# Attention weights cast to bf16 in DRAM first, and loaded by SP's queue instead of GpSimd's

## The chip, the cores and the metric

One Trainium2 chip, all 8 cores. Each core runs the same program on its own data: core 2b + half computes 1024 of the 2048 tokens of batch element b, and reads the whole sequence for keys and values. There is no traffic between cores. The metric is the device time of one execution in microseconds, that of the slowest core; lower is better.

## The reference

One adaLN transformer layer on x of shape (4, 2048, 2048), float32, 16 heads of 128, MLP of 8192 with ternary weights and 8-bit activations:

```python
mod = (_silu(L0_c) @ L0_wmod).reshape(L0_c.shape[0], 6, 1, -1)
sa, ca, ga, sb, cb, gb = (mod[:, 0], ..., mod[:, 5])
ga = (2 * (ga >= 0) - 1) * jnp.maximum(jnp.abs(ga), 0.25)      # gb likewise
h = _layernorm(x, axis=-1) * (1 + ca) + sa
x = x + ga * attn(h, wq, wk, wv, wo)      # rope on q and k, softmax over 2048 keys, y @ wo.T
h = _layernorm(x, axis=-1) * (1 + cb) + sb
x = x + gb * ffn(h, w1, w2, w3)
# ffn: bitlinear(h, w) = rmsnorm, activations rounded to 8 bits by their row's maximum,
#      weights rounded to -1, 0, 1 by the mean of |w|;
#      silu(bitlinear(h, w1)) * bitlinear(h, w2), then bitlinear(., w3)
```

## The kernel before

The kernel is written by hand, engine by engine. `st(engine, fn, waits, inc)` (L63) appends an instruction to the engine's list; `waits` are semaphores with the value to wait for, `inc` is what it raises when done. The five lists run in the order in which they were written (L81). VectorE (DVE) and ScalarE (ACT) also count every instruction of their own (sVE, sSE), sMM counts finished groups of matmuls. A DMA is issued by SyncE (its queue is SPq in the profile, the hardware queue q1) or by GpSimd (POOL, the software queue q0); a wait holds all that stands behind it on the same engine. In this kernel every DMA that changes float32 into bf16 is issued by POOL, all others by SP.

The stages, in order:

1. POOL issues 16 loads of x (xc, 1 MB of float32 each, cast into h_sb, L289), then the first weight loads. DVE meanwhile makes the rope tables.
2. Modulation (L369 to L412): for j in 24 groups of 512 columns of wmod, 16 loads of 256 KB (L378) go into the ring mring, which has two halves of 8 loads; TensorE multiplies them in float32 (L396), DVE picks the diagonal (L408, L411). A half is loaded again when its matmuls are done.
3. First layer norm over 4 blocks of tokens (L440 to L508): sums on TensorE, the rows sent round by a bounce through DRAM on SP (`bounce`, L230), DVE and ACT write h into h_sb.
4. 16 heads, in the order of `events` (L609): V of two heads ("V", g), then ("KQ", 2g), ("KQ", 2g+1). Event i uses slot i % 2 (wsl or wsl2, 8 KB per partition). The load of event i + 2 (`emit_ev_load`, L623) waits until the last matmul of event i is done; it is written right behind that event's matmuls, L682 and L760. After K and Q of head h (L692, L728; the copy out on ACT, L704 and L738) comes `emit_scale(24)` (L574, called at L772): 24 chunks of 512 KB of w1, w2 or w3, each loaded by SP in two DMAs (L592) into one of three slots (halves of wfl, rbc), and summed by ACT as |w| (L599); 16 x 24 chunks are all three matrices. Then the attention of the head: scores (L795), exp on ACT (L806), sums and P V (L779, L785). A chunk's load waits for ACT's sum of the chunk three before it.
5. The softmax sums go through DRAM and are spread to all partitions, one load per head into rbc or sm2 (L846), and DVE scales ysb (L854).
6. Output projection for 16 blocks dc of 128 outputs (L888): SP loads the block of x into xst (L892), the weights come by `emit_wo_load` (L874) into two slots, the load of dc + 2 waits for wo_done[dc], the last statistics matmul (L937) of block dc. 2 x 16 matmuls (L902), ACT scales (L911), DVE adds x (L917) and casts (L921), TensorE sums x and its square (L933, L937), SP spills the block (x2s, L946).
7. Second layer norm, quantization, the MLP with w1, w2 (L1184, L1195), and w3 (L1396). These parts load their weights on SP.

Of the kernel before, what the change touches and what calls it, by code (L numbers as in the profile page):

```python
# [7 lines left out]
BF16 = mybir.dt.bfloat16  # L8
# [6 lines left out]
NKC = D // 128  # L15
# [27 lines left out]
class Bld:  # L43
# [19 lines left out]
    def st(self, eng, fn, waits=(), inc=None, inck=1):  # L63
        ser = self.serial.get(eng)
        if ser is not None:
            waits = tuple(waits) + ((ser, ser.n),)
            inc, inck = ser, 1
        waits = tuple((s.h, v) for (s, v) in waits if v > 0)
        if inc is not None:
            inc.inc(inck)  # L70

        def run(e, fn=fn, waits=waits, inc=inc, inck=inck):
            for h, v in waits:
                e.wait_ge(h, v)
            r = fn(e)
            if inc is not None:
                r.then_inc(inc.h, inck)
        self.q[eng].append(run)
        return inc.n if inc is not None else None
# [12 lines left out]
def build(nc, dbg=(), phases=99, e_head=0):  # L92
    dbg = set(dbg)
    K = Bld(nc)
    st = K.st
# [3 lines left out]
    cvec_d = nc.dram_tensor("cvec", [128, NKC], F32, kind="ExternalInput").ap()  # L99
    pos_d = nc.dram_tensor("pos", [1, T], F32, kind="ExternalInput").ap()  # L100
    wmod_d = nc.dram_tensor("wmod", [24, 128, NKC, 512], F32, kind="ExternalInput").ap()
    wq_d = nc.dram_tensor("wq", [NH, 128, NKC, 128], F32, kind="ExternalInput").ap()
    wk_d = nc.dram_tensor("wk", [NH, 128, NKC, 128], F32, kind="ExternalInput").ap()
    wv_d = nc.dram_tensor("wv", [8, 128, NKC, 256], F32, kind="ExternalInput").ap()
    wo_d = nc.dram_tensor("wo", [NKC, 128, NKC, 128], F32, kind="ExternalInput").ap()
# [87 lines left out]
    sM1 = K.sem("sM1")  # L193
    sST0 = K.sem("sST0")
    sST1 = K.sem("sST1")
    sB = [K.sem("sB%d" % i) for i in range(6)]
    sVE = K.sem("sVE")
    sSE = K.sem("sSE")
    sMM = K.sem("sMM")
# [40 lines left out]
    def emit_ladder(chains):  # L240
# [31 lines left out]
        out=t_ang[:, :], in_=pos_d[0:1, :].broadcast_to((64, T))), inc=sLD, inck=16)  # L272
# [15 lines left out]
    for kc in range(NKC):  # L288
        st("gpsimd", lambda e, kc=kc: e.dma_start(  # L289
            out=h_sb[:, kc * T:(kc + 1) * T], in_=xc[kc * 128:(kc + 1) * 128, :]),  # L290
           inc=sXL, inck=16)
    w_xall = sXL.n

    st("scalar", lambda e: e.activation(out=tab[:, 2:3], in_=tab[:, 1:2], func=AF.Ln),
       waits=[(sVE, w_consts)])
# [13 lines left out]
    for k in [256.0, 128.0, 64.0, 32.0, 16.0, 8.0, 4.0, 2.0, 1.0]:  # L309
# [27 lines left out]
       waits=[(sVE, w_sinin)])  # L337
# [285 lines left out]
    def emit_ev_load(ev):  # L623
        i = ev_index[ev]
        sl = slot_of[ev]
        sA = sAs[sl]
        wcred = [(sMM, ev_done[events[i - 2]])] if i >= 2 else []
        if i == 1:
            wcred = wcred + [(sSE, w_cos)]
        if ev[0] == "V":  # L630
            g = ev[1]
            st("gpsimd", lambda e, sl=sl, g=g: e.dma_start(
                out=slots[sl][:, 0:4096], in_=wv_d[g]), waits=wcred, inc=sA, inck=16)
        else:
            h = ev[1]
            st("gpsimd", lambda e, sl=sl, h=h: e.dma_start(
                out=slots[sl][:, 0:2048], in_=wk_d[h]), waits=wcred, inc=sA, inck=16)
            st("gpsimd", lambda e, sl=sl, h=h: e.dma_start(
                out=slots[sl][:, 2048:4096], in_=wq_d[h]), inc=sA, inck=16)
        ev_ld[ev] = sA.n  # L640

    emit_ev_load(events[0])
# [231 lines left out]
    def emit_wo_load(dc):  # L874
        sl = dc % 2
        sA = sAs[sl]
        st("gpsimd", lambda e, dc=dc, sl=sl: e.dma_start(
            out=wo_slot[sl], in_=wo_d[dc]),
           waits=[(sMM, wo_done[dc - 2])] if dc >= 2 else
                 [(sMM, ev_done[events[-2 + dc]])], inc=sA, inck=16)  # L880
        ev_ld[("WO", dc)] = sA.n

    emit_wo_load(0)
# [617 lines left out]
```

How the kernel before makes its waits and increments, by code:

```python
        def run(e, fn=fn, waits=waits, inc=inc, inck=inck):  # L72
            for h, v in waits:
                e.wait_ge(h, v)
            r = fn(e)
            if inc is not None:
                r.then_inc(inc.h, inck)
```

## Time and profile before

| what | us |
|---|---|
| timed runs, median of 2 (8291.23 to 8309.24) | 8300.23 |
| the profiled execution's own time | 8325.77 |
| its span on the slowest core (cores: 8259.1 to 8324.2) | 8324.2 |
| TensorE / VectorE / ScalarE / GpSimd busy | 3580.1 / 2874.6 / 3055.9 / 38.9 |
| moved by DMA | 706.67 MB |

The span is the time from the first to the last instruction of core 1 in one profiled execution. Busy times of the engines overlap each other; a matmul's end is modelled. Times below are counted from the span's start. "x16" behind a row says that so many instructions were merged, and a bracket tells how long the engine was idle before it and what released it. GB/s and MB count the bytes that are written, so a cast from float32 counts half of what it reads.

### The profile page before, as it was taken

The numbers are of one execution on the slowest core, as the hardware profiler recorded it, in microseconds if no ns is written. First come the engines' busy times: TensorE is split into PE (matmuls) and PEld (weight loads), VectorE is DVE, ScalarE is ACT, GpSimd is POOL, SyncE is SP. The second block draws the span as 40 slices with busy tenths as digits, with TensorE's granted clock in tenths as the row PEclk, the third lists the DMA queues.
The fourth block names the chain that finished last, engine by engine and source line by source line (L and its number), as shares of the span: only waits on it lengthen the run. The fifth ranks groups of instructions, "written<-read, shape, count | busy, mean of one in ns | idle before, by whom it ended". The sixth has DMA issues, their size and how long they took to land.

```text
span 8324.2 us, 57853 instructions; the slowest of 8 cores (8259.1 to 8324.2 us)
## 1 busy us (share of the span) xinstructions
PE 3580.1 (43%) x12896; PEld 1437.6 (17%) x12896; DVE 2874.6 (35%) x4177; ACT 3055.9 (37%) x4011; POOL 38.9 (0%) x76
## 2 busy tenths in 40 slices
PE   4872454545364436003565656651111111154544
PEld 1330222212221112001222222220000000011111
DVE  4225211122121211584333333336666666411111
ACT  0003343343334411264333333334555555422222
POOL 0000000000000000000000000000000000000000
PEclk9775787778787767556777778775555555576677
DMA  7650424243324423201222222211011111133333
GB/s 196 196 150 16 122 86 126 77 129 100 108 80 130 124 73 84 71 1 46 82 89 84 87 86 85 90 62 33 31 34 32 33 34 31 62 104 107 104 106 106
DMA packets 442896, 706.67 MB, mean 85 GB/s; under 512 B 50307, under 2 KB 197766, under 8 KB 441472
## 3 DMA queue, kind: packets, MB, share of 16 engines
q1 hardware_dynamic: 432192, 661.04, 25.6%
q0 software_dynamic: 10368, 41.95, 2.9%
q8 instruction: 114, 1.87, 0.1%
q14 instruction: 222, 1.82, 0.1%
HBM read 693.97 MB, written 50.51 MB: 89 GB/s over the span
## 4 chain that ended last, share of the span: by engine, by line
ACT 24%; DVE 24%; DMA 20%; PE 16%; issue 9%; SPq 5%; DVEq 1%; ACTq 1%
DMA wfl<-w 13%; DVE sm L256 6%; ACT tmpb L250 6%; PE ps L396 5%; PE ps L1396 4%; ACT esb L806 4%; PE ps L665 3%; DMA rbc<-w 3%; DVE ternB L1167 2%; PE ps L902 2%; ACT sgntmp L1160 2%; ACT terntmp L1153 2%; ACT sgntmp L1157 2%; ACT sgntmp L1162 2%; ACT terntmp L1365 1%
## 5 line engine op out<-in xcount | busy, mean ns | idle before, releaser
L1396 PE MATMUL ps<-q3c,ternA 128*128 128x512 bf16 x2048 | 766.8, 553 | 1934.1 <-DVE ternA L1373 1934.0
L250 ACT ACTIVATE tmpb<-sm,consts 128x512 f32<-128x512 f32 x1120 | 808.4, 722 | 173.5 <-DVE sm L256 119.4
L256 DVE SCALAR_TENSOR_TENSOR sm<-tmpb,sm 128x512 f32<-128x512 f32 x1120 | 774.5, 692 | 206.8 <-ACT tmpb L250 135.6
L1184 PE MATMUL ps<-q,ternA 128*128 128x512 bf16 x2048 | 570.7, 448 | 360.7 <-DVE ternB L1167 360.7
L1396 PEld LDWEIGHTS ps<-q3c,ternA 128*128 128x128 bf16 x2048 | 255.7, 130 | 2445.2 <-issue 2396.6
L1365 ACT ACTIVATE terntmp<-wfl,wsc 128x512 f32<-128x512 f32 x256 | 184.7, 721 | 1144.0 <-DMA wfl<-w 1051.2
L795 PE MATMUL ps<-qsb,ksb 128*128 128x512 bf16 x512 | 209.3, 420 | 900.1 <-ACT esb L806 811.9
L1373 DVE TENSOR_TENSOR ternA<-terntmp,sgntmp 128x512 bf16<-128x512 f32 x256 | 177.3, 693 | 1191.3 <-ACT sgntmp L1370 1191.3
L396 PE MATMUL ps<-mring,smt 128*128 128x512 f32 x768 | 431.1, 731 | 149.5 <-DVE smt L388 131.4
L1195 PE MATMUL ps<-q,ternB 128*128 128x512 bf16 x2048 | 452.5, 379 | 0.0
L1164 DVE TENSOR_TENSOR ternA<-terntmp,sgntmp 128x2048 bf16<-128x2048 f32 x64 | 146.7, 2293 | 797.5 <-ACT sgntmp L1157 735.3
L819 DVE COPY rows<-ps 1x512 f32<-1x512 f32 x32 | 21.7, 679 | 1114.7 <-PE ps L795 836.9
L599 ACT ACTIVATE wfl<-wfl 128x1024 f32<-128x1024 f32 x256 | 270.4, 1056 | 325.0 <-DMA wfl<-w 317.8
L806 ACT ACTIVATE esb<-ps,consts 128x512 bf16<-128x512 f32 x512 | 351.8, 687 | 79.8 <-PE ps L795 36.5
L1234 PE MATMUL ps<-sqb,onesb 128*128 128x512 bf16 x128 | 74.8, 584 | 685.5 <-ACT sqb L1226 685.5
L1184 PEld LDWEIGHTS ps<-q,ternA 128*128 128x128 bf16 x2048 | 228.6, 113 | 690.9 <-issue 530.4
L1153 ACT ACTIVATE terntmp<-wfl,wsc 128x2048 f32<-128x2048 f32 x64 | 128.1, 2002 | 581.9 <-DMA wfl<-w 575.1
L665 PE MATMUL ps<-wsl,h_sb 128*128 128x256 bf16 x2048 | 262.1, 275 | 136.0 <-DVE vsb L676 89.9
L704 ACT ACTIVATE kraw<-ps 128x512 f32<-128x512 f32 x64 | 38.2, 597 | 598.9 <-PE ps L692 398.6
L692 PE MATMUL ps<-h_sb,wsl 128*128 128x512 bf16 x1024 | 231.3, 379 | 51.6 <-ACT kraw L704 51.6
L1195 PEld LDWEIGHTS ps<-q,ternB 128*128 128x128 bf16 x2048 | 200.4, 98 | 241.6
L795 PEld LDWEIGHTS ps<-qsb,ksb 128*128 128x128 bf16 x512 | 51.2, 102 | 1099.1 <-issue 1093.5
(199 smaller groups left out, 4612.0 us busy)
## 6 DMA issues: line engine op xcount, KB each, us to landing
wfl<-w SPq DMA_DIRECT2D x1024, 256.0 KB, 4.5
mring<-wmod SPq DMA_DIRECT2D x384, 256.0 KB, 4.6
rbc<-w SPq DMA_DIRECT2D x256, 256.0 KB, 4.5
wfl<-w SPq DMA_DIRECT2D x512, 128.0 KB, 2.3
q3c<-q3s SPq DMA_DIRECT2D x384, 128.0 KB, 2.2
xst<-x2s SPq DMA_DIRECT2D x32, 512.0 KB, 3.8
hs<-hch SPq DMA_DIRECT2D x128, 128.0 KB, 1.7
hch<-hs SPq DMA_DIRECT2D x128, 128.0 KB, 2.4
```

What stands on the lines that cost most here:

```text
L250: sws[j] = st("scalar", lambda e, ch=ch, src_u=src_u: e.activation(out=ch["bb"], in_=src_u, func=AF.Sign, bias=consts[:, 8:9]), waits=[(sV ...
L256: e.scalar_tensor_tensor(out=ch["tb"], in0=ch["bb"], scalar=-(k / 2.0), in1=src_u, op0=ALU.mult, op1=ALU.add),
L396: st("tensor", lambda e, j=j, kc=kc, kk=kk, hs=hs, sl2=sl2: e.matmul(psE[:, :], sl2, mring[:, (hs % 2) * 4096 + kk * 512: (hs % 2) * 4096 ...
L599: "scalar", lambda e, slot=slot, col=col: e.activation(out=slot, in_=slot, func=AF.Abs, accum_out=accw[:, col:col + 1]),
L665: st("tensor", lambda e, kkc=kkc, kc=kc, sl=sl_v: e.matmul(psE[:, 0:256], h_sb[:, kc * T + kkc * 128: kc * T + kkc * 128 + 128], slots[sl] ...
L795: qslot=qslot: e.matmul(ps_s[:, 0:512], kslot[:, kkc * 128:(kkc + 1) * 128], qslot[:, qh * 512:(qh + 1) * 512], start=True, stop=True),
L806: w_exp[(h, qh, kkc)] = st("scalar", lambda e, kkc=kkc, ps_s=ps_s: e.activation(out=esb[:, kkc * 512:(kkc + 1) * 512], in_=ps_s[:, 0:512], ...
L1153: st("scalar", lambda e, wslc1=wslc1: e.activation(out=terntmp[:, :], in_=wslc1[:, :], func=AF.Sign, bias=wsc[:, 6:7]), waits=[(sW, w_wld) ...
L1184: e.matmul((psU0 if th == 0 else psU1)[:, 0:512], tA[:, kc * 128:(kc + 1) * 128], q12[:, kc * OWN + th * 512: kc * OWN + (th + 1) * 512], ...
L1195: st("tensor", lambda e, th=th, kc=kc, tB=tB: e.matmul((psC if th == 0 else psD)[:, 0:512], tB[:, kc * 128:(kc + 1) * 128], q12[:, kc * OW ...
L1365: st("scalar", lambda e, wslc=wslc: e.activation(out=terntmp[:, 0:512], in_=wslc[:, 0:512], func=AF.Sign, bias=wsc[:, 6:7]), waits=[(sW, w ...
L1396: tsl=tsl: e.matmul(psx[:, 0:512], tsl[:, di * 128:(di + 1) * 128], qsl[:, th * 512:(th + 1) * 512], start=(k3 == 0), stop=(k3 == NFC - 1)),
```

## The change

All attention weights are first cast to bf16 by DMAs from DRAM to DRAM: 56 casts, issued by POOL right behind the loads of x, into four new DRAM tensors. The loads of the weights into SBUF are then plain bf16 loads, issued by SP, and each of them waits for all 56 casts (sPC) as well as for its slot. They are written at the same places as before, so on SP they now stand between the instructions that SP already had there.

```diff
+    wvbf_d = nc.dram_tensor("wvbf", [8, 128, 4096], BF16, kind="Internal").ap()
+    wkbf_d = nc.dram_tensor("wkbf", [16, 128, 2048], BF16, kind="Internal").ap()
+    wqbf_d = nc.dram_tensor("wqbf", [16, 128, 2048], BF16, kind="Internal").ap()
+    wobf_d = nc.dram_tensor("wobf", [16, 128, 2048], BF16, kind="Internal").ap()
...
@@ -290,6 +295,25 @@
     w_xall = sXL.n
+
+    def _pc(dst, srcv):
+        st("gpsimd", lambda e, dst=dst, srcv=srcv: e.dma_start(out=dst, in_=srcv),
+           inc=sPC, inck=16)
+        pc_n[0] += 1
+
+    for g in range(8):
+        _pc(wvbf_d[g], wv_d[g])
+        for h in (2 * g, 2 * g + 1):
+            _pc(wkbf_d[h], wk_d[h])
+            _pc(wqbf_d[h], wq_d[h])
+    for dc in range(NKC):
+        _pc(wobf_d[dc], wo_d[dc])
@@ -624,19 +648,20 @@
-        wcred = [(sMM, ev_done[events[i - 2]])] if i >= 2 else []
+        wcred = ([(sMM, ev_done[events[i - 2]])] if i >= 2 else []) + \
+                [(sPC, 16 * pc_n[0])]
         if i == 1:
             wcred = wcred + [(sSE, w_cos)]
         if ev[0] == "V":
             g = ev[1]
-            st("gpsimd", lambda e, sl=sl, g=g: e.dma_start(
-                out=slots[sl][:, 0:4096], in_=wv_d[g]), waits=wcred, inc=sA, inck=16)
+            st("sync", lambda e, sl=sl, g=g: e.dma_start(
+                out=slots[sl][:, 0:4096], in_=wvbf_d[g]), waits=wcred, inc=sA, inck=16)
         else:
             h = ev[1]
-            st("gpsimd", lambda e, sl=sl, h=h: e.dma_start(
-                out=slots[sl][:, 0:2048], in_=wk_d[h]), waits=wcred, inc=sA, inck=16)
-            st("gpsimd", lambda e, sl=sl, h=h: e.dma_start(
-                out=slots[sl][:, 2048:4096], in_=wq_d[h]), inc=sA, inck=16)
+            st("sync", lambda e, sl=sl, h=h: e.dma_start(
+                out=slots[sl][:, 0:2048], in_=wkbf_d[h]), waits=wcred, inc=sA, inck=16)
+            st("sync", lambda e, sl=sl, h=h: e.dma_start(
+                out=slots[sl][:, 2048:4096], in_=wqbf_d[h]), inc=sA, inck=16)
@@ -874,10 +899,11 @@
-        st("gpsimd", lambda e, dc=dc, sl=sl: e.dma_start(
-            out=wo_slot[sl], in_=wo_d[dc]),
-           waits=[(sMM, wo_done[dc - 2])] if dc >= 2 else
-                 [(sMM, ev_done[events[-2 + dc]])], inc=sA, inck=16)
+        st("sync", lambda e, dc=dc, sl=sl: e.dma_start(
+            out=wo_slot[sl], in_=wobf_d[dc]),
+           waits=([(sMM, wo_done[dc - 2])] if dc >= 2 else
+                  [(sMM, ev_done[events[-2 + dc]])]) +
+                 [(sPC, 16 * pc_n[0])], inc=sA, inck=16)
```

Three places, as the built programs have them (lines of the changed kernel are some 5 to 26 higher than those of the kernel before). First POOL's list at the start. Before:

```order
L289 DMA h_sb<-xc 128x2048 x16
L632 DMA wsl<-wv 128x4096
L636 DMA wsl_100<-wk 128x2048 [waits sSE]
L638 DMA wsl_100<-wq 128x2048
L636 DMA wsl<-wk 128x2048 [waits sMM]
```

And now:

```order
L294 DMA h_sb<-xc 128x2048 x16
L303 DMA wvbf<-wv 32x16384
L303 DMA wkbf<-wk 16x16384
L303 DMA wqbf<-wq 16x16384
L303 DMA wkbf<-wk 16x16384
L303 DMA wqbf<-wq 16x16384
L303 DMA wvbf<-wv 32x16384
```

wsl_100 is the second slot, wsl2. The loads into the slots are gone from POOL, and the casts stand in their place without any wait, each as 16 or 32 runs of 16384 elements.

Second, SP's list between the attention of one head (L822, now L847, sends its sums out) and the scale chunks of the next (L592, now L616), where the next head is an even one. Before:

```order
L592 DMA rbc<-w 128x512 [waits sSE]
L592 DMA rbc<-w 128x512
L822 DMA bnc<-rows 1x1024 [waits sVE]
L592 DMA wfl<-w 128x512 [waits sSE]
L592 DMA wfl<-w 128x512
L592 DMA wfl<-w 128x512 [waits sSE]
```

And now:

```order
L616 DMA rbc<-w 128x512 [waits sSE]
L616 DMA rbc<-w 128x512
L847 DMA bnc<-rows 1x1024 [waits sVE]
L661 DMA wsl_100<-wkbf 128x2048 [waits sMM,sPC]
L663 DMA wsl_100<-wqbf 128x2048
L657 DMA wsl<-wvbf 128x4096 [waits sMM,sPC]
L616 DMA wfl<-w 128x512 [waits sSE]
L616 DMA wfl<-w 128x512
L616 DMA wfl<-w 128x512 [waits sSE]
```

Weight loads that wait for matmuls (sMM) of V and of K and Q now stand ahead of the first scale chunks; before an odd head it is one such load pair.

Third, SP's list in the output projection. Before:

```order
L892 DMA xst<-xc 128x1024 [waits sVE,sXS0]
L946 DMA x2s<-xst 128x1024 [waits sVE]
L892 DMA xst<-xc 128x1024 [waits sVE,sXS1]
L946 DMA x2s<-xst 128x1024 [waits sVE]
L892 DMA xst<-xc 128x1024 [waits sVE,sXS0]
```

And now:

```order
L918 DMA xst<-xc 128x1024 [waits sVE,sXS0]
L902 DMA wsl<-wobf 128x2048 [waits sMM,sPC]
L972 DMA x2s<-xst 128x1024 [waits sVE]
L918 DMA xst<-xc 128x1024 [waits sVE,sXS1]
L902 DMA wsl<-wobf 128x2048 [waits sMM,sPC]
L972 DMA x2s<-xst 128x1024 [waits sVE]
```

A wo load with a wait for TensorE now stands ahead of each spill and of the next load of x.

## Rows read from the trace of the kernel before

**Rows 1.** The page: busy time by engine; the chain that ended last.

```profile
PE 3580.1 (43%) x12896; PEld 1437.6 (17%) x12896; DVE 2874.6 (35%) x4177; ACT 3055.9 (37%) x4011; POOL 38.9 (0%) x76
ACT 24%; DVE 24%; DMA 20%; PE 16%; issue 9%; SPq 5%; DVEq 1%; ACTq 1%
```

**Rows 2.** Stages: length, busy of PE, PEld, DVE, ACT, POOL, PEclk, DMA share, GB/s.

```profile
86.00:587.00 501.00, 436.52 (x787) 169.76 (x787) 143.61 (x437) 3.24 (x8) 0.54 (x2) 0.79 0.65 195
587.00:815.00 228.00, 54.44 (x109) 12.75 (x109) 117.18 (x156) 94.10 (x130) 0.00 (x0) 0.52 0.05 14
```

**Rows 3.** Waits (total us, times, longest), and the landing of loads into wsl.

```profile
PE ps L396 <- DMA mring<-wmod: 18.0, 6, 4.4
...
POOL wsl L636 <- PE ps L665: 1661.6, 8, 773.1
...
DMA to landing us min/median/max: 5.1/7.1/69.0
```

**Rows 4.** DMA at the start: queues 10 to 70 us (packets, MB, share); mring loads to 75 us; h_sb loads.

```profile
q0 software_dynamic: 2101, 7.72, 75.2%
q1 hardware_dynamic: 2091, 4.11, 27.3%
...
mring<-wmod SPq DMA_DIRECT2D x16, 256.0 KB, 39.7
...
L289 POOL DMA_DIRECT2D h_sb<-xc x16: 535/606/662, 1.6 to 9.5; - x16
DMA to landing us min/median/max: 7.8/35.8/62.8
```

**Rows 5.** Chain of the modulation stage; the line of its matmuls.

```profile
265.89 18.39 PE ps L396 x32
286.75 18.39 PE ps L396 x32
...
L396 PE MATMUL ps<-mring,smt x768: 592/698/1193, 86.0 to 579.9; 128*128 128x512 f32 x192
```

**Rows 6.** DMA issues from 200 to 580 us: KB each, median us to landing.

```profile
mring<-wmod SPq DMA_DIRECT2D x279, 256.0 KB, 4.5
```

**Rows 7.** Timeline at the end of the first layer norm.

```profile
815.36 1.80 PE L665 MATMUL ps<-wsl,h_sb 128*128 128x256 bf16 x7 [45.69 <-ACT tab L509]
```

**Rows 8.** One head's scale chunks: timeline; two stretches (columns as rows 2); sums in wfl.

```profile
2342.10 0.53 POOL L636 DMA_DIRECT2D wsl<-wk  x1 [129.86 <-PE ps L728]
2342.63 1.06 ACT L599 ACTIVATE wfl<-wfl 128x1024 f32<-128x1024 f32 x1
2351.46 1.06 ACT L599 ACTIVATE wfl<-wfl 128x1024 f32<-128x1024 f32 x1 [5.20 <-DMA wfl<-w]
2394.37 2.26 ACT L806 ACTIVATE esb<-ps,consts 128x512 bf16<-128x512 f32 x3
...
2341.60:2394.30 52.70, 1.01 (x2) 0.14 (x2) 3.50 (x7) 28.17 (x49) 1.15 (x2) 0.53 0.77 229
2370.00:2376.00 6.00, 0.00 (x0) 0.00 (x0) 0.00 (x0) 3.45 (x6) 0.00 (x0) 0.50 0.83 267
...
L599 ACT ACTIVATE wfl<-wfl x256: 1056/1056/1057, 887.7 to 2907.9; 128x1024 f32<-128x1024 f32 x128
```

**Rows 9.** Output projection: timeline of block 0 into 1; landing and waits for xst.

```profile
3042.35 6.57 PE L902 MATMUL ps<-ysb,wsl 128*128 128x512 bf16 x16 [94.55 <-DVE ysb L854]
3060.54 0.33 SPq L892 DMA_DIRECT2D xst<-xc  x1
3061.89 0.53 POOL L877 DMA_DIRECT2D wsl<-wo  x1 [199.90 <-PE ps L937]
3067.57 0.69 DVE L917 TENSOR_TENSOR xst<-xst,kraw 128x512 f32<-128x512 f32 x1 [7.86 <-ACT kraw L911]
...
DMA xst<-xc: 29.9, 4
...
DMA to landing us min/median/max: 2.6/4.0/7.3
```

More of the change, by code:

```diff
@@ L195, in build @@
     sST1 = K.sem("sST1")
+    sPC = K.sem("sPC")
     sB = [K.sem("sB%d" % i) for i in range(6)]
@@ L292, in build @@
     w_xall = sXL.n
+    pc_idx = {}
+    pc_n = [0]
+    def _pc(dst, srcv):
[4 more added lines that the diff above has]
+        _pc(wvbf_d[g], wv_d[g])
+        pc_idx[("V", g)] = pc_n[0]
+        for h in (2 * g, 2 * g + 1):
+            _pc(wkbf_d[h], wk_d[h])
+            _pc(wqbf_d[h], wq_d[h])
+            pc_idx[("KQ", h)] = pc_n[0]
+    for dc in range(NKC):
+        _pc(wobf_d[dc], wo_d[dc])
+        pc_idx[("WO", dc)] = pc_n[0]
     st("scalar", lambda e: e.activation(out=tab[:, 2:3], in_=tab[:, 1:2], func=AF.Ln),
```

## The prediction

> **What bounds the kernel now.** I read the shares of the engines and the chain that ended last, then the waits by engine, then the stages one by one, and last the DMA rows of the stages that the change touches. No engine carries the span: TensorE is busy for 43% of it, and the chain runs through ACT, DVE, DMA and PE in turn [rows 1]. What counts is which wait ends last in each stage. Of the stages, the change touches the modulation matmuls (86 to 587 us) with the layer norm behind them (587 to 815) [rows 2], the heads (815 to 3042, the weight scales among them) [rows 7, 9], and the output projection (3042 to 3323). The 5001 us behind them (8324 less 3323: MLP and what leads to it) keep their instructions.
>
> The question to ask first is whether anybody waits for the loads that are changed. In the list of what TensorE waits for [rows 3] no row names a load of wsl; the only DMA in it is mring, with 18.0 us. Turned round, it is POOL that waits for TensorE to free a slot, for the K loads alone 1661.6 us behind V's matmuls [rows 3]. Such a load lands in 7.1 us (median) [rows 3] and is asked for two events ahead. Making it cheaper can't shorten a wait that isn't there. What can change is the traffic that the casts add, and what the loads do to the queue into which they are moved.
>
> **Part 1: 56 casts from DRAM to DRAM at the start.** They write 8 x 2 MiB / 2 + 48 x 0.5 MiB = 32 MiB = 33.55 MB of bf16 and read twice that. Price per MB: from 10 to 70 us the old kernel does nearly nothing on its DMA engines but the same kind of transfer (xc cast into h_sb). There the software queue moved 7.72 MB in 75.2% of 16 engines' time [rows 4], so 60 x 0.752 / 7.72 = 5.84 us of all 16 engines per MB. The casts cost 33.55 x 5.84 = 196 us of all 16. They queue behind the 16 xc loads, the last of which is issued at 9.5 us and lands 62.8 us later, at 72 [rows 4]; the wv load that came next (69.0 us to landing) is gone. The matmuls begin at 86.0 us, so some 13 us or 2.2 MB are free; 31.3 MB (183 us) are left, beside the loads of wmod.
>
> That stage has no room for 183 us. One j (16 loads of 256 KB, 4.19 MB; the matmuls of 16 k-chunks) takes 20.86 us: it starts at 265.89, the next at 286.75 [rows 5]. The DMA engines are 0.65 busy meanwhile [rows 2]. The ring holds only one j ahead, so loads that come too slowly stop TensorE. How the two queues share is shown from 10 to 70 us too: beside the casts the hardware queue got 27.3% and moved 4.11 MB in 60 us [rows 4], against 12.1 MB that the stage wants in that time. By these rates the casts need 31.3 / 7.72 x 60 = 243 us, in which wmod advances by 243 x 4.11 / 60 = 16.7 MB, 4.0 j, where it made 243 / 20.86 = 11.7 before. Lost: 7.7 x 20.86 = 160 us. The other end of sharing is that the wmod loads get nearly nothing while a cast is there: the order of the changed kernel shows each cast as 16 or 32 pieces of 16384 elements, where h_sb has rows of 2048. Then the loss is the 183 us. I take 175, nearer to this end, since the pieces are eight times as long as those of the row. Bounds: if the casts only fill gaps it is 0 (35% of 501 us and nearly all of 228 us are idle [rows 2], 391 us in all, so they would fit); if writing to DRAM makes them 1.5 times as long, 249 (worked out below). No row of this trace shows DRAM to DRAM.
>
> The Trainium skill ("DMA: Bandwidth & Descriptors", Queues, rings and completion order) says that each DMA engine takes turns between its queues by whole packets. By that rule the casts don't step back for loads that are awaited, and large pieces would push the loss to the 183 us end; the 27.3% beside 75.2% [rows 4] agree with taking turns.
>
> That every later head waits for all 56 casts costs nothing: they are through by 329 us (86 + 243; by 418 in the slow rival below), and the first load that needs them is issued by SP behind the layer norm's last broadcast, while DVE and ACT still write h; TensorE can't use it before h is done at 815.36 [rows 7], and both move by the same delay.
>
> **Part 2: the loads of a head, now on SP, ahead of the scale chunks.** Per head SP also loads 24 chunks of 512 KB for ACT's sums of |w| (L592, L599), three slots deep, and ACT must be through with them before the head's first exp, since it works in order. Before, SP fetched the first three as soon as the attention of the head before was done, so ACT took them without a wait when its last K/Q copy was done, at 2342.63, and the fourth came at 2351.46 [rows 8]. Now SP stands at the load of the next event, which waits for this head's last Q matmul; the first three chunks are queued behind it and can't be prefetched. Worked out on that head: SP wakes at about 2342.0 as POOL does now (2342.10), two issues take 0.7, 1.05 MB of bf16 pass at about 260 GB/s (267 in the stretch from 2370 [rows 8]) in 4 us, the first chunk's 0.5 MB in 2, and landing adds 2: the first chunk is there at 2350.5. From there 24 chunks are to do, where before 21 were left at 2351.46, done at 2394.3, when the exps begin: 42.8 / 21 = 2.04 us each [rows 8]. New end 2350.5 + 24 x 2.04 = 2399.5, against 2394.3: 5.2 us, less some 0.5 because no cast competes with the refills. I take 4.7 per head; all 16 heads have such a batch (ACT's sums in wfl, two of the three slots, are 256 = 16 x 16 [rows 8]), so 75 us. Bounds: 3 chunks and the weights' own 4 us, 10 per head or 160; and -1 per head (-16) if the halved weight traffic gave back all of it, because the first refills, which now share with the cast, wait 5.20 us [rows 8]. The value is nearer to the refill rows, since each step has a row.
>
> A weight load itself is not late: what it waits for is unchanged and its use is a head later.
>
> **Part 3: the output projection.** There SP now issues, ahead of the spill of block dc and the load of block dc+1 of x, a wo load that waits for the block's last statistics matmul. Before: spill, then the x load at 3060.54, its user (L917) ready at 3067.57; POOL's own wake by the same matmul is at 3061.89 [rows 9]. Now: wake 3061.8, wo issue, spill, x load at about 3062.8, 2.3 us later, with 0.5 MB more ahead of it (2 us). Median landing is 4.0, so it lands at 3068.8, against 3067.4: 1.4 us late, some 15 times: 20 us. Bounds 0 and 70 (landing 7.3, the largest seen, makes it 4.7 late); in the old kernel four already came late, 29.9 us of waiting [rows 9]. The first two wo loads now stand right behind the last broadcast of softmax sums, and their use at 3042.35 waits for the DVE operation that needs this broadcast [rows 9]; so the first lands about when it is wanted: at nothing, up to 2.
>
> **Removed:** 40 loads and 16 wo loads with cast from POOL. Nobody waited, POOL has nothing else; 0, apart from the half microsecond counted in part 2.
>
> **Sum.** 175 + 75 + 20 = 270 us on the profiled execution's 8325.8, whose span is 8324.2. It lies 25.6 above the 8300.2 median of the timed runs, so the forecast for a timed run is 8570 us, 3.3% slower.
>
> **Rivals.**
> - *The writes to DRAM slow the casts.* From 10 to 70 us casts wrote to SBUF; now each 2 bytes read cost 1 byte written to the memory that is being read. If reads and writes add up, a cast takes 1.5 times as long. On top of 7.72 MB's 75.2 parts of engine time come 37.6: 243 us become 243 x 140.1 / 102.5 = 332, wmod still makes 4.0 j, where 15.9 went before: 11.9 x 20.86 = 249 (rounded). Time 8300 + 249 + 95 = 8644. For it: 7.72 MB of casts are 15.4 MB read, with the other queue's 4.11 that is 326 GB/s of reading, where loads without a cast run at 267 [rows 8]; against: the queues' shares add up to 102.5% [rows 4], so the engines may be the limit and not the memory. The Trainium skill ("HBM Reference", Specifications) gives about 358 GB/s per core with both of a pair at work; by it 100.7 MB would take 281 us (an estimate), and the loss would be near this rival's. No run here shows it. 25%.
> - *The casts fit into the gaps.* If the loads of wmod are served ahead of the casts, part 1 is 0, and the time is 8300 + 95 = 8395: within 2%, not slower. For it: 391 us of idle engine time before 815 us; against: the 16 first mring loads, beside casts, took 39.7 us each (median) where 4.5 is usual [rows 4, 6]. It decides from the point where part 1 is under 71 us (166 less 95). If besides the lighter refills give back part 2, it ends at 8304. 12%.
> - *SP's place costs nothing in the heads* (the chunks come in bursts, ACT catches up): part 2 is 0, 8495. For it: ACT takes a chunk in 1.06 us and idles otherwise. Against: the engines are 0.77 busy in this stretch [rows 8], so lost prefetch is lost transfer time. 8%.
>
> **How the numbers follow.** Forecast 55% (8570, own range 8490 to 8630), slow writes 25%, gaps 12%, heads free 8%. A measurement tells about 2% from no change, here 166 us: slower means over 8466. Faster by over 2% has no case of its own: 1%, taken from the gaps rival's 12%, whose other 11% are within 2%; the other three are slower, 88%. The range goes from 8440 (below it lies most of the gaps rival) to 8720 (slow writes with the upper ends of parts 2 and 3).
>
> **What would show it.** Right: the matmuls of L396 end some 175 us later than 580, with mring as what they wait for, and the DMA share is near 1.0 up to about 330 us; layer norm as long as before; the wait for the first chunk of each head is 7 to 8 us where there was none, and no 5 us wait behind the third; L917 waits for xst in most blocks; the stages from 3323 on are as long as before. Wrong: matmuls of L396 at their old pace, heads as long as before, or a wait of TensorE for wsl, which would mean that a weight load on SP is late.

## The result, and the profile after

The changed kernel takes 8684.84 us (median of 11 runs), the kernel before, timed beside it, 8314.26 (10 runs). The ratio is 1.0429, 95% interval 1.0395 to 1.0463: about 357 us slower at 8314. The medians are over all runs, the ratio is over those in which neither half of the chip's cores ran late at a lower clock. The forecast was 270 us and slower; the sign and the three places were right, the size of the largest term was not.

I cut each core's span at four events that the profile gives for every core (first and last start of a matmul line), and took means over the eight cores. "mod" ends with the last modulation matmul, "LN" with the first matmul of V, "heads" with the first matmul of the output projection, "proj" with the first matmul of the MLP (the second layer norm and the quantization are in it).

| mean of 8 cores, us | mod | LN | heads | proj | rest | span |
|---|---|---|---|---|---|---|
| before | 551.0 | 231.3 | 2225.3 | 781.1 | 4498.7 | 8287.5 |
| after | 832.5 | 233.2 | 2263.0 | 802.5 | 4499.0 | 8630.3 |
| difference | +281.5 | +1.9 | +37.7 | +21.4 | +0.3 | +342.8 |
| forecast | +175 | 0 | +75 | +20 | 0 | +270 |

The mean matters here, since the slowest core is another one than before: core 1 then, core 7 now. Core 7's modulation ended at 526.1 before and at 865.8 after. The rows of the profile after are those of core 7.

The page first, the lines that answer to [rows 1], with the slices of the clock and of the DMA:

```profile
PE 3611.3 (42%) x12896; PEld 1443.9 (17%) x12896; DVE 2876.2 (33%) x4177; ACT 3064.0 (35%) x4011; POOL 44.0 (1%) x76
PEclk7577577877878776755788777776555555566776
DMA  9977023334232342210122222221111101133333
...
ACT 23%; DVE 23%; DMA 20%; PE 15%; issue 8%; SPq 6%; another core or an unknown queue 3%; DVEq 1%; ACTq 1%
```

No compute engine has noticeably more to do. The page's lines on DRAM traffic, before and now:

```profile
HBM read 693.97 MB, written 50.51 MB: 89 GB/s over the span
```

```profile
HBM read 727.53 MB, written 84.06 MB: 94 GB/s over the span
```

The casts read 67.1 MB and write 33.55, and the bf16 loads give back 33.55 of reading: the change adds 67.1 MB of traffic in all. The DMA line starts with two slices (433 us) at 0.9 or more, which is where the casts run.

Modulation, first from the timeline of PE:

```profile
120.16 10.29 PE L420 MATMUL ps<-mring,smt 128*128 128x512 f32 x16 [25.42 <-DMA mring<-wmod]
313.04 10.04 PE L420 MATMUL ps<-mring,smt 128*128 128x512 f32 x16 [182.60 <-DMA mring<-wmod]
390.79 8.72 PE L420 MATMUL ps<-mring,smt 128*128 128x512 f32 x16 [67.70 <-DMA mring<-wmod]
```

and from three stretches, with columns as in [rows 2]:

```profile
200.00:300.00 100.00, 0.00 (x0) 0.00 (x0) 0.00 (x0) 0.00 (x0) 0.00 (x0) 0.50 1.00 117
300.00:400.00 100.00, 18.76 (x32) 7.04 (x32) 4.26 (x15) 0.00 (x0) 0.00 (x0) 0.56 0.93 130
400.00:500.00 100.00, 83.57 (x147) 32.88 (x148) 27.84 (x84) 0.00 (x0) 0.00 (x0) 0.77 0.71 190
```

From 200 to 300 us TensorE does nothing at all, at full DMA share. What TensorE waited for in mring was 18.0 us [rows 3]; now the list of waits has it at 303.4 us (over the eight cores 18.0 to 99.8 before, 301.7 to 356.4 now). From 400 us the pace is the old one. The DMA queues in the stretch from 100 to 200 us (packets, MB, share of 16 engines):

```profile
q0 software_dynamic: 588, 10.68, 94.7%
q1 hardware_dynamic: 586, 1.07, 5.3%
```

The waits of PE (idle us, how many, the longest):

```profile
PE ps L420 <- DMA mring<-wmod: 303.4, 12, 182.6
```

And the line that issues the casts, those of wk and the last ones, of wo; the landing is that of all 56:

```profile
L303 POOL DMA_DIRECT2D wkbf<-wk x16: 486/566/1371, 10.5 to 34.2; - x16
L303 POOL DMA_DIRECT2D wobf<-wo x16: 486/486/1336, 36.0 to 44.8; - x16
DMA to landing us min/median/max: 70.7/212.1/341.9
```

These rows say three things. The last cast is issued at 44.8 us and lands 341.9 later, at 387; the casts fill the engines from 72 to there. Their price is 0.947 x 100 x 16 / 10.68 = 142 engine us per MB written, where the same division on [rows 4] gives 93.5. And wmod moves 1.07 MB in 100 us, a quarter of one j: both queues show about the same number of packets (588 and 586), but 10.68 MB of the casts' are some 326 pieces of 32 KB (the rest are under 512 B), and wmod's are rows of 2 KB.

Heads, one odd head, from the timeline of SP and ACT; the rows answer to [rows 8]:

```profile
2659.62 0.33 SPq L661 DMA_DIRECT2D wsl<-wkbf  x1
2660.00 0.42 SPq L663 DMA_DIRECT2D wsl<-wqbf  x1
2660.52 2.43 SPq L616 DMA_DIRECT2D wfl<-w  x4
...
2666.98 1.06 ACT L623 ACTIVATE wfl<-wfl 128x1024 f32<-128x1024 f32 x1 [6.52 <-DMA wfl<-w]
2714.97 2.26 ACT L831 ACTIVATE esb<-ps,consts 128x512 bf16<-128x512 f32 x3
```

The prefetch is gone as forecast: SP issues the first chunks only behind the weight loads, and ACT stands 6.52 us for the first one, where it had no wait. From there to the exps it is 48.0 us for 24 chunks, 2.00 each. Over all heads and the mean of the eight cores, ACT waited 449.1 us for the chunks' loads, against 409.0 before; these 40 us make up the 37.7 that the heads got longer.

Projection, one block of the timeline of SP and DVE; the rows answer to [rows 9]:

```profile
3399.70 0.32 SPq L902 DMA_DIRECT2D wsl<-wobf  x1
3400.64 0.33 SPq L918 DMA_DIRECT2D xst<-xc  x1
3406.79 0.69 DVE L943 TENSOR_TENSOR xst<-xst,kraw 128x512 f32<-128x512 f32 x1 [8.79 <-DMA xst<-xc]
```

and the waits of DVE in this stage:

```profile
DVE xst L943 <- DMA xst<-xc: 119.5, 14, 9.1
```

The load of x is what DVE waits for here: such waits were 4, with 29.9 us of idle time of DVE ended by them [rows 9], and are 14, with 119.5 (mean of the cores: 21.0 and 116.7). Not all of it is added to the stage, since the same operation's waits for ACT fell meanwhile, from 210.4 us on core 1 to 138.2 on core 7.

### The profile page after: what moved, and what is told of

It is laid out like the page before. It is cut to its first block, busy times and chain, and to the rows that moved or that the text cites. A ratio compares the mean times of both kernels' runs of the same rounds, so it can differ in the third digit from the quotient of the medians.

```text
span 8664.6 us, 57949 instructions; the slowest of 8 cores (8577.0 to 8664.6 us)
## 1 busy us (share of the span) xinstructions
PE 3611.3 (42%) x12896; PEld 1443.9 (17%) x12896; DVE 2876.2 (33%) x4177; ACT 3064.0 (35%) x4011; POOL 44.0 (1%) x76
## 4 chain that ended last, share of the span: by engine, by line
ACT 23%; DVE 23%; DMA 20%; PE 15%; issue 8%; SPq 6%; another core or an unknown queue 3%; DVEq 1%; ACTq 1%
DMA wfl<-w 12%; DVE sm L261 6%; ACT tmpb L255 5%; PE ps L420 4%; PE ps L1422 4%; DMA rbc<-w 4%; ACT esb L831 4%; PE ps L690 3%; DVE ternB L1193 2%; ACT sgntmp L1186 1%; ACT terntmp L1179 1%; ACT sgntmp L1183 1%; ACT sgntmp L1188 1%; ACT terntmp L1391 1%
## 5 line engine op out<-in xcount | busy, mean ns | idle before, releaser
L1422 PE MATMUL ps<-q3c,ternA 128*128 128x512 bf16 x2048 | 786.9, 564 | 1921.9 <-DVE ternA L1399 1921.9
L261 DVE SCALAR_TENSOR_TENSOR sm<-tmpb,sm 128x512 f32<-128x512 f32 x1120 | 775.8, 693 | 207.4 <-ACT tmpb L255 136.7
L420 PE MATMUL ps<-mring,smt 128*128 128x512 f32 x768 | 442.1, 746 | 424.4 <-DMA mring<-wmod 303.4
L623 ACT ACTIVATE wfl<-wfl 128x1024 f32<-128x1024 f32 x256 | 270.6, 1057 | 343.4 <-DMA wfl<-w 338.6
L412 DVE TENSOR_SCALAR smt<-onesf,modv 128x128 f32<-128x128 f32 x384 | 110.0, 286 | 595.7 <-PE ps L420 587.9
L420 PEld LDWEIGHTS ps<-mring,smt 128*128 128x128 f32 x768 | 173.3, 232 | 692.1 <-issue 670.3
L717 PE MATMUL ps<-h_sb,wsl 128*128 128x512 bf16 x1024 | 231.3, 379 | 51.6 <-ACT kraw L729 51.6
```

The source lines that it names most:

```text
L261: e.scalar_tensor_tensor(out=ch["tb"], in0=ch["bb"], scalar=-(k / 2.0), in1=src_u, op0=ALU.mult, op1=ALU.add),
L420: st("tensor", lambda e, j=j, kc=kc, kk=kk, hs=hs, sl2=sl2: e.matmul(psE[:, :], sl2, mring[:, (hs % 2) * 4096 + kk * 512: (hs % 2) * 4096 ...
L623: "scalar", lambda e, slot=slot, col=col: e.activation(out=slot, in_=slot, func=AF.Abs, accum_out=accw[:, col:col + 1]),
L717: st("tensor", lambda e, tkc=tkc, kc=kc, sl=sl_kq: e.matmul(pst, slots[sl][:, kc * 128:(kc + 1) * 128], h_sb[:, kc * T + tkc * 512: kc * T ...
L1422: tsl=tsl: e.matmul(psx[:, 0:512], tsl[:, di * 128:(di + 1) * 128], qsl[:, th * 512:(th + 1) * 512], start=(k3 == 0), stop=(k3 == NFC - 1)),
```

## The experiments

Each ratio is against the kernel before, timed beside that run on the same chip (medians 8345.5, 8349.2 and 8316.7 us); stages are means over the eight cores, cut as above, of one profiled execution each.

| | mod | LN | heads | proj | rest | ratio (95%) |
|---|---|---|---|---|---|---|
| casts_only | 853.9 | 232.1 | 2228.5 | 775.9 | 4504.5 | 1.0358 (1.0286 to 1.0430) |
| pool_loads | 843.0 | 231.9 | 2194.2 | 775.6 | 4501.8 | 1.0303 (1.0251 to 1.0356) |
| sp_reordered | 838.3 | 232.7 | 2176.9 | 780.5 | 4503.3 | 1.0281 (1.0204 to 1.0357) |
| small_pieces | 836.9 | 231.2 | 2276.3 | 811.7 | 4494.2 | 1.0429 (1.0385 to 1.0474) |
| casts_to_sbuf | 714.1 | 230.3 | 2226.7 | 775.8 | 4512.1 | 1.0218 (1.0146 to 1.0289) |
| stores_only | 609.6 | 229.8 | 2226.9 | 776.0 | 4480.8 | 1.0079 (1.0038 to 1.0120) |
| late_long | 535.4 | 408.1 | 2164.0 | 777.4 | 4503.7 | 1.0150 (1.0103 to 1.0198) |
| late_short | 552.2 | 356.3 | 2175.2 | 775.9 | 4500.5 | 1.0057 (1.0021 to 1.0093) |
| paced | 621.8 | 296.7 | 2233.7 | 790.7 | 4495.1 | 1.0077 (1.0038 to 1.0116) |
| shifted | 543.2 | 229.7 | 2155.1 | 774.1 | 4487.5 | 0.9936 (0.9896 to 0.9976) |

What a difference between two of these rows is worth shows where instructions are the same. Heads of before, casts_only, casts_to_sbuf and stores_only: 2225.3 to 2228.5. Projection of the same four: 775.8 to 781.1, the kernel before being the high one. Modulation of before, late_long, late_short and shifted: 535.4 to 552.2, and of the four kernels with the changed kernel's casts (after, casts_only, pool_loads, sp_reordered) 832.5 to 853.9.

**casts_only: the casts without the new loads.**

```diff
-            st("sync", lambda e, sl=sl, g=g: e.dma_start(
-                out=slots[sl][:, 0:4096], in_=wvbf_d[g]), waits=wcred, inc=sA, inck=16)
+            st("gpsimd", lambda e, sl=sl, g=g: e.dma_start(
+                out=slots[sl][:, 0:4096], in_=wv_d[g]), waits=wcred, inc=sA, inck=16)
```

and the same for wk, wq, wo, without the wait for sPC.

> The 56 casts stay, but the weights are loaded as before the change (from float32, by POOL), so nothing reads the copies. In the changed kernel the mean over the cores of the last modulation matmul is 832.5 us (551.0 before), the heads last 2263.0 (2225.3), the stretch from the output projection to the first MLP matmul 802.5 (781.1). If the loss of modulation is the casts' alone and that of heads and projection is SP's order alone: modulation ends near 832, heads back at 2225, the stretch at 781, ratio to the kernel before 1.034. Rival, the casts disturb later stages too (clock, memory): heads or projection stay above by 10 us or more.

Measured: modulation 853.9, heads 2228.5, projection 775.9. The loss of modulation belongs to the casts alone, that of heads and projection not at all.

**pool_loads: bf16 loads, but from POOL.**

```diff
-            st("sync", lambda e, sl=sl, g=g: e.dma_start(
+            st("gpsimd", lambda e, sl=sl, g=g: e.dma_start(
                 out=slots[sl][:, 0:4096], in_=wvbf_d[g]), waits=wcred, inc=sA, inck=16)
```

> The changed kernel with the bf16 loads issued by POOL again instead of SP, same waits. SP's order as the cause: heads fall from 2263 to 2225 or, since half the bytes are read beside the scale chunks, some 1 us per head less (2209); projection stretch from 802.5 to 781 or a few less; modulation stays near 832; ratio 1.032. Rival, the loads themselves are at fault (a plain bf16 load of 4 KB rows is slow or lands late): heads and projection stay at 2263 and 802.

Measured: heads 2194.2, projection 775.6. So SP's list costs 69 us in the heads and 27 in the projection, and the bf16 loads themselves give back 31 in the heads (2225.3 to 2194.2). In the projection they give nothing that can be seen: 775.6 here, 775.9 in casts_only with loads from float32. The 69 us are 4.3 per head, where my gross term was 5.2, and the gift of 31 us (2 per head) is four times what I allowed (0.5).

**sp_reordered: on SP, but behind what is urgent.** The first three chunks' loads are emitted at the end of a head, behind L847 (`emit_scale` then takes these three as loaded), and a wo load behind the next x load:

```diff
+        prefetch_scale(3)
...
-        if dc + 2 < NKC:
-            emit_wo_load(dc + 2)
...
         w_xo = sXO.n
+        if 1 <= dc and dc + 1 < NKC:
+            emit_wo_load(dc + 1)
```

> The changed kernel, loads still on SP, but SP's list rearranged: the first three scale chunks of a head are asked for before the weight loads, and a wo load stands behind the next x load. If only the place in SP's list costs time, heads and projection come to what they are with the loads on POOL (2194 and 776, from 2263 and 802), modulation stays near 832: ratio 1.030. Rival, sharing SP's hardware ring with the chunks costs by itself: heads stay above 2225.

Measured: heads 2176.9, projection 780.5. Nothing is wrong with SP's ring as such; the place in the list was the cost. That the heads are 17 us shorter than with POOL's loads wasn't expected. It lies in the same wait: ACT waited 356.8 us for the chunks' loads (mean of the cores), against 381.8 in pool_loads. Why the chunks come sooner when the weight loads stand in their own queue isn't shown. Cores 6 and 7 stand at 2206.7 and 2196.5, the others at 2161 to 2175; their waits are no longer (353.2 and 347.4), but their granted clock in the heads was 0.74 and 0.75, against 0.78.

**small_pieces: the same casts in rows.**

```diff
-    wkbf_d = nc.dram_tensor("wkbf", [16, 128, 2048], BF16, kind="Internal").ap()
+    wkbf_d = nc.dram_tensor("wkbf", [16, 128, 2056], BF16, kind="Internal").ap()
...
-            _pc(wkbf_d[h], wk_d[h])
+            _pc(wkbf_d[h][:, 0:2048], wk_d[h])
```

> The changed kernel with padded rows in the four bf16 tensors, so that a cast is 128 rows of 2048 (wv: 4096) elements instead of 16 or 32 runs of 16384. Two causes are claimed for modulation's 281 us: long pieces starve the wmod loads (turns), and writing to DRAM makes a cast 1.5 times as long (142 instead of 93.5 engine us per MB). If both: casts still take 1.5 times as long, but wmod advances by about 4 j meanwhile instead of 1; modulation is late by about 249, ends near 800. If the length of the casts is the long pieces' fault and not the DRAM write's: 160 late, ends near 711. If piece size means nothing: 832 as before.

Measured: 836.9, the end of the long pieces, although 800 was expected. The queues from 100 to 200 us:

```profile
q0 software_dynamic: 1918, 8.56, 79.2%
q1 hardware_dynamic: 1900, 3.47, 20.2%
```

Again one packet for one packet (1918 and 1900), and now wmod gets 3.47 MB in 100 us instead of 1.07. So turns by packet are shown. But the casts take longer in return (the last lands 417.3 us after its issue instead of 341.9; 148 engine us per MB), wmod's loads are dearer too (0.202 x 100 x 16 / 3.47 = 93 engine us per MB, where [rows 4] gives 64), and the sum is the same. Here the piece size decided who waited, and not how long both took. (The padded loads also made the heads 13 us longer and the projection 9.)

**casts_to_sbuf and stores_only: the price taken apart.** The first casts the same bytes into SBUF:

```diff
+    for n, srcv in enumerate(srcs):
+        sd = sD[n % 8]
+        st("gpsimd", lambda e, n=n, srcv=srcv: e.dma_start(out=dslots[n % 8], in_=srcv),
+           waits=[(sd, sd.n)], inc=sd, inck=16)
```

> 64 casts of the same bytes (33.55 MB of bf16), but into eight 4 KB slots of SBUF that are not used yet, each waiting for the one eight before; nothing reads them, and the weights are loaded as before the change. If the DRAM write makes the casts long: 93.5 engine us per MB again, modulation late by some 160 us, ends near 711. Rival, long casts come from something else (the second part of the weights, contention between the cores): 142 per MB and the end near 800, as small_pieces.

Measured: modulation ends at 714.1, against 711 expected. Its rows are 4 KB, as most of small_pieces' are, and the queues are as full; what differs is where the casts write, and that is worth 123 us. The second run only writes:

```diff
+    for n in range(64):
+        dst = (wkbf_d, wqbf_d, wobf_d, wvbf_d)[n // 16][n % 16][:, 0:2048]
+        st("gpsimd", lambda e, n=n, dst=dst: e.dma_start(
+            out=dst, in_=h_sb[:, (n % 16) * T:(n % 16 + 1) * T]),
+           waits=([(sXL, w_xall)] if n == 0 else []), inc=sPC, inck=16)
```

> No casts; in their place 64 plain stores of the same 33.55 MB of bf16 from h_sb to DRAM, in rows of 4 KB, issued by POOL when h_sb is loaded; nothing reads them, and the weights are loaded as before the change. It prices the write alone. If a cast to DRAM costs the sum of its read (93.5 engine us per MB written) and its write, a store costs 142 - 93.5 = 48.5 or somewhat more, so about 102 us of all engines; modulation late by some 70 to 85 us, ends near 630. If a store costs much less than 48.5, the sum is no explanation and the casts pay for something else; if 90 or more, writes of DRAM are slow by themselves.

Measured: modulation ends at 609.6, 59 late, somewhat less than the 70 to 85 expected. The queues, first of casts_to_sbuf from 100 to 200 us, then of stores_only from 80 to 150 us:

```profile
q0 software_dynamic: 3568, 13.00, 76.2%
q1 hardware_dynamic: 3563, 6.49, 25.7%
```

```profile
q0 software_dynamic: 4808, 17.51, 80.1%
q1 hardware_dynamic: 2843, 5.19, 23.4%
```

A cast into SBUF costs 0.762 x 100 x 16 / 13.00 = 93.8 engine us per MB, a store 0.801 x 70 x 16 / 17.51 = 51.2. Together 145, and the cast from DRAM to DRAM costs 142 (148 in rows). The write to DRAM is the missing third. The packets of stores_only are unequal (4808 and 2843) because wmod's queue was empty up to 100 us; from 110 to 120 they are 602 and 602.

**late_long and late_short: the casts in the layer norm.** On top of sp_reordered the casts wait for the end of modulation, and each load for its own group:

```diff
     w_mod = sVE.n
+    emit_casts(56, waits=[(sVE, w_mod)])
...
-                [(sPC, 16 * pc_n[0])]
+                [(sPG[ev[1] if ev[0] == "V" else ev[1] // 2], 80)]
```

> sp_reordered, with all 56 casts issued only when modulation is done, in the layer norm, whose DMA engines are 0.05 busy; each weight load waits for its own group of casts. Modulation must be back at 551. The casts need 300 us, the layer norm lasts 231 without them and sends 8 rows round, each a load of 128 rows, 8 per engine. If the engines take turns by piece and a cast's piece lasts 4.65 us, each such load takes some 37 us: layer norm 231 to about 400, heads 2194, projection 776, ratio about 1.016. Rival, small loads get through beside long pieces: layer norm at most 245, ratio 0.998.

> late_long with padded rows, so that a cast's piece is a row of 2048 or 4096 elements (0.6 or 1.2 us). By turns: each broadcast takes some 5 us more, layer norm 231 to about 270; the last casts run beside the first head, where DMA is idle; ratio about 1.000. Rival, the casts take the engines whatever their pieces: layer norm as long as in late_long.

Measured: modulation is back (535.4, 552.2), heads and projection keep what sp_reordered gave, and the layer norm pays: 408.1 and 356.3 instead of 231.3 (about 400 and 270 were expected). Of late_long, first the DMA issues from 560 to 780 us (the last number is the median from issue to landing), then the waits from 560 to 1000:

```profile
rbc<-bnc SPq DMA_DIRECT2D x4, 256.0 KB, 32.0
```

```profile
DVE sm L520 <- DMA rbc<-bnc: 216.8, 4, 81.2
```

and the same two of late_short:

```profile
rbc<-bnc SPq DMA_DIRECT2D x4, 256.0 KB, 18.3
```

```profile
DVE sm L520 <- DMA rbc<-bnc: 163.1, 4, 42.8
```

In the kernel before, this load landed in 3.1 us, and DVE waited 36.6 us for it in all. A load that is small itself (8 rows per engine) took 32.0 us, about seven of its neighbour's pieces at 4.65 us; eight, or 37, were expected. The short pieces disappointed (18.3 us, where I had allowed 5 more than 3.1), and the rival, that the casts take the engines whatever their pieces, was nearer. What I had left out: each block sends two rows round, each by a write and a read one behind the other, and each of the four steps waits. In late_short:

```profile
620.30 0.30 SPq L237 DMA_DIRECT2D bnc<-rows  x1
628.95 0.36 SPq L240 DMA_DIRECT2D rbc<-bnc  x1
629.39 0.61 SPq L237 DMA_DIRECT2D bnc<-rows  x1
647.38 0.33 SPq L240 DMA_DIRECT2D rbc<-bnc  x1
662.97 0.69 DVE L520 TENSOR_TENSOR sm<-h_sb,rbc 128x512 f32<-128x512 bf16 x1 [42.74 <-DMA rbc<-bnc]
```

A read is issued when its write has landed. From the first write to the second read it is 27.1 us here; in the kernel before it was 4.3 (607.44 to 611.71).

**paced: casts in small doses.**

```diff
         wmm = sMM.n
+        emit_casts(1, waits=[(sMM, wmm)])
```

> late_short, but 24 of the 56 casts (14.5 of 33.6 MB, 129 us of all engines at the rate measured) are issued one per j of modulation, when its matmuls are done; the stage has 175 us of idle engine time. If idle time can be used when the casts come in small doses: modulation 551 to 575, layer norm about 255, ratio 0.998 to 1.003. If a dose delays the wmod loads behind which it falls by its whole length: modulation 551 to 680, ratio 1.012.

Measured: modulation 621.8, so 24 casts cost 71 us, between the two guesses, and layer norm 296.7, where about 255 was expected. (The 24 casts write 15.2 MB, not 14.5, which makes the upper guess 135 us instead of 129.) Part of the 71 is the clock. In this execution it was low on all cores, 0.672 to 0.691 over the span. Cores 0, 1, 6 and 7, with 0.76 or 0.77 in modulation, end it at 617 to 632; in the kernel before, cores 0 and 1, with 0.78 and 0.79, end at 582 and 580. That leaves some 35 to 50 us for the casts, which need 135 us of all engines: the gaps can be used, but in part only.

The heads took 2233.7, 57 more than sp_reordered with the same instructions, and that is the clock too. ACT's waits for the chunks are the same (357.2 and 356.8 us), the granted clock in the heads is 0.715 against 0.77, and TensorE is busy for 1117.7 us against 1050.3 (means of the cores). Nothing ties this to the kernel: other executions of paced had 0.70 to 0.71 over the span, and took 8374 to 8393 us where the profiled one took 8467.

**shifted: the kernel before, with its loads moved in time.** If the bf16 loads saved 31 to 48 us in the heads because the scale chunks have less traffic beside them, the casting load can simply be kept away from them, with no copy in DRAM:

```diff
-        ni = ev_index[kq_ev] + 2
-        if ni < len(events):
-            emit_ev_load(events[ni])
...
         emit_scale(24)
+        ni = ev_index[kq_ev] + 2
+        if ni < len(events):
+            emit_ev_load(events[ni], [(sSE, scale_state["se"][scale_state["i"] - 1])])
```

> The kernel before, without any cast in DRAM: loads cast from float32 by POOL, but the one that used to start at a head's last Q matmul, beside the scale chunks, now also waits until ACT has summed the head's 24 chunks, and so runs beside the attention, where DMA is idle. With bf16 loads kept out of the way, heads took 2177 (sp_reordered) to 2194 (pool_loads) against 2225. If what these saved is contention with the scale chunks, all of the load's 5.9 us of engine time per head leaves this stretch: heads 2225 to about 2145, the rest as before, ratio 0.990. Rival, the saving came from something that only bf16 loads have: heads stay at 2225, ratio 1.000. If a load comes too late for its matmuls, TensorE would show waits for wsl.

Measured: heads 2155.1 (70 less; 2145 expected), ratio 0.9936, interval 0.9896 to 0.9976. It is faster than both kernels, than the kernel before by 0.6%, which is little but clear of the noise. TensorE shows no wait for wsl. What ACT waits for in the scale chunks, here:

```profile
ACT wfl L599 <- DMA wfl<-w: 250.6, 188, 24.2
ACT rbc L599 <- DMA rbc<-w: 107.9, 91, 17.3
```

358.5 us in all, on core 6. The same two rows gave 317.8 and 90.0 in the kernel before (407.8, core 1), and 338.6 and 119.9 in the changed one (458.5, core 7). These are the slowest cores; the means over all eight, beside the length of the heads:

| mean of 8 cores, us | before | after | casts_only | pool_loads | sp_reordered | shifted |
|---|---|---|---|---|---|---|
| ACT waits for chunk loads | 409.0 | 449.1 | 414.3 | 381.8 | 356.8 | 340.4 |
| heads | 2225.3 | 2263.0 | 2228.5 | 2194.2 | 2176.9 | 2155.1 |

Against the kernel before, the heads gain or lose, within 4 us, what this one wait gains or loses.

## Why the prediction was right or wrong

*The total.* 8570 us were forecast and 8684.84 measured. That is inside the range of 8440 to 8720, but above the 8490 to 8630 that the forecast case gave itself, and nearest to the 8644 of the rival "the writes to DRAM slow the casts", which had 25%. That the sum was no further off is partly luck: part 1 was 106 us too small and part 2 was 37 too large.

*Nobody waits for the weight loads.* Right in the heads: no load of wsl appears there among TensorE's waits in any of the kernels, on any core, and casts_only loses nothing where it loads as before. The one exception is the start of the projection: on one core each of after, sp_reordered and late_short the first wo load came last of what the first matmul waited for, in a pause of 96.4 to 99.8 us that is 94.5 us in the kernel before. The forecast had allowed up to 2 us there.

*Part 1, 175 us; measured 281.5.* Mechanism and place right, the term mis-sized, and the step that failed is the price per MB: 5.84 us of all 16 engines, taken from casts that write to SBUF. Measured 142 / 16 = 8.9. I had this as the rival "the writes to DRAM slow the casts", with 25% and 249 us; the runs bear it out, and its factor of 1.5 was right too (142 / 93.5 = 1.52). Its 249 was still short, because there I let wmod make 4.0 j during the casts, at the share and the price of [rows 4]. With pieces of 32 KB wmod made about one: 315 us of casts (72 to 387), less the 13 before the matmuls begin, less one j of 21, is 281. The starving is not what makes the difference, though. In small_pieces wmod did get its share, some 3 j in 390 us, and modulation ended at 836.9 all the same: a j at 93 engine us per MB takes all engines for 24.4 us, more than the 20.86 that TensorE needs for it. The loss is nearly the casts' own time at the measured price, as if no gap were used: 33.55 x 8.9 = 298, less 13, is 285 (281.5 measured); for small_pieces 33.55 x 9.25, less 13, is 297 (285.9 measured). The decision for the fast price hung on "the queues' shares add up to 102.5%, so the engines may be the limit": full engines don't tell what fills them.

The two queues had equal counts of packets, 588 and 586, and 1918 and 1900. The Trainium skill ("DMA: Bandwidth & Descriptors", Queues, rings and completion order) says that each engine takes turns between its queues by whole packets; the trace agrees.

Why the price is reading plus writing shows when both are added. In 100 us the casts move 33.1 MB to and from DRAM (3 x 10.68 + 1.07), casts_to_sbuf 32.5 (2 x 13.00 + 6.49), and stores_only 22.7 in 70 us (17.51 + 5.19): 331, 325 and 324 GB/s, and 326 on [rows 4]. The agreement isn't perfect: small_pieces stays under them with 291, at engines just as full, and stores_only, from 80 to 90 us, when it had the engines to itself, wrote 3.56 MB, 356 GB/s. The Trainium skill ("HBM Reference", Specifications) gives about 358 GB/s per core with both cores of a pair at work; the mixed runs come out on the sum of both directions, some 7 to 10% below that figure. Whether DRAM is the limit or the engines' own data paths, no run here tells apart.

*The gaps rival* is out: with 391 us of idle time before 815, a queue that is full still takes every second turn. Two ways of using the gaps were tried, small doses (paced) and the layer norm (late_short); neither gets below the time before.

*Part 2, 75 us; measured 37.7.* The wait at the head's start was forecast as 7.9 us from 2342.63 and is 6.5, and 2.04 us per chunk came out as 2.00. What failed most is the credit of "some 0.5 because no cast competes": pool_loads shows 31 us for 16 heads, 1.9 each. SP's order costs 69 us, 4.3 each, where 5.2 was worked out. Of the 37 us that were too much, some 22 are the credit's and 15 the order's. Loads cast from float32 stood beside the scale chunks at the one time of the head when DMA is what ACT waits for. This was visible in the wait of 5.20 us [rows 8], which I used for the lower bound only.

*Part 3, 20 us; measured 21.4.* Right in its mechanism: the x load behind the wo load became what DVE waits for in 14 blocks instead of 4. Against pool_loads (775.6) the order costs 27. The 5 us between that and the kernel before (781.1) can't be credited to the smaller loads, since casts_only, casts_to_sbuf and stores_only stand at 775.8 to 776.0 with loads from float32; so the size is 21 to 27, and that it met the forecast within 2 is better than this can be measured.

*Stages behind 3323 us*: 4498.7 and 4499.0, as forecast.

## What to carry to other kernels

Before making a load cheaper, look whether anybody waits for it, and then what it runs beside: here the load's cost lay in the time that it took from a neighbour. Halving the bytes that it reads gave back 1.9 us per head, moving it in time 4.4, without a copy. Price a copy from DRAM to DRAM by what it reads plus what it writes, and add it to the traffic of the stage in which it runs: idle DMA time in a stage is not free for a queue that is full, since it takes turns with the queue that is urgent. When loads are moved to another engine's list, look at each instruction that then stands behind the moved one's wait; the prefetch was lost by order alone, and came back by order alone.

## What the runs showed of the hardware that was not expected

- The price of a DMA by direction, in us of one of the 16 engines per MB written: 93.8 for a cast from DRAM to SBUF, 51.2 for a store, 142 for a cast from DRAM to DRAM. The sum of the first two is within 3% of the third. (All beside the loads of wmod, on all eight cores.)
- A contiguous copy between DRAM tensors is cut into 16 or 32 pieces of 32 KB written, and a queue of such pieces held a queue of 2 KB rows at 1.07 MB in 100 us, against 3.47 beside pieces of 4 and 8 KB.
- A load of 8 rows per engine took 32.0 us beside the long pieces and 18.3 beside the short ones, against 3.1 alone.
- The end of modulation differs by core already in the kernel before, from 525.7 to 582.3 us, with the same instructions, and the granted clock goes with most of it. Cores 0 and 1, which end last, had 0.78 and 0.79 and a median matmul of 698 ns; cores 2 and 7, which end first, had 0.94 and 592 ns. After the change the ends are 799.8 to 865.8, in another order of the cores, and cores 6 and 7, which end last, had 0.76 from 400 us on.
